# A bidirectional scan with routed experts on one core: the common mark behind the preparation is taken out, and three rows of C are read ahead of the expert rows

## The chip, the core and the metric

The kernel runs on one core of one Trainium2 chip. A core has TensorE (PE, matmuls), VectorE (DVE), ScalarE (ACT), GpSimd (POOL) and SyncE (SP), each with an instruction stream of its own, tied by semaphores. SP issues nearly all DMAs here; POOL issues the indirect ones. The metric is the device time in microseconds of one execution; the median of the runs is compared.

## The reference

The input x is 8 sequences of 512 tokens with 128 features, in float32. It is normalized per token (xn), and two branches are added to x:

```python
xn = layernorm(x)
# branch 1: two state-space scans, one forwards, one on the reversed sequence
xz = einsum('ed,bld->bel', in_proj_w, xn)           # x, z: 256 channels each
u = silu(causal_conv(x, 4 taps) + bias)             # per direction
delta = softplus(dt_proj(x_proj(u)[:8]) + dt_bias); B, C = x_proj(u)[8:24], [24:40]
h[l] = exp(delta * A) * h[l-1] + delta * B * u      # 16 states per channel
y = sum_n(h * C) + D * u;  out = y * silu(z)        # both directions added
branch1 = out_proj(out_f + out_b)
# branch 2: 16 experts, the best 4 of each token
logits = -|xn - keys|^2 + xn @ rw + rb;  top 4, softmax weights
branch2 = sum_k w_k * (w2_e @ gelu(w1_e @ xn + b1_e) + b2_e)
return x + branch1 + branch2
```

## The kernel before, in words

There is a preparation of all 8 batches, and then 8 batches of scans, each of 32 steps (`PAIRS`, q = 0 to 31).

**The preparation.** `prepare(b)` exists on ACT, PE and DVE. It makes, per batch, delta (`pos_part`, two halves), du = delta * u (`du_p`), the gate, the skip term, and the rows of B (parts) and C. These are stored to memory arrays delta_d, du_d, gate_d, skip_d, parts_d and c_d by SP (`store_prepared`, L614 and L622), and each store counts up a semaphore: delta_out, du_out, gate_out, skip_out, parts_out, c_out. Meanwhile POOL scatters the token rows to slots sorted by expert (L817).

**The arena.** Most working arrays of both phases are carved out of one array `arena`, so that the second phase writes where the first one had its arrays. `decay` (a ring of 8 steps) lies over constants, the transposed xn and weights. `c_rows` (a ring of 4) lies over weights, `mag` and, with the fourth slot and a little of the third, `pos_part` and its neighbour. The states lie over u, the rows of B and C and `fit`. The du of the second batch parity is `du_p`'s memory in part.

**The border.** At the end of `prepare(BATCH - 1)` DVE writes eight memsets into `decay` (the column where a scan starts, L1527) and marks them with decay_free, for which ACT waits ahead of its first decay. Then DVE waits for the last stores of gate, C, parts and delta, for skip_sb and du_ready, and sets one semaphore, `prepared`. It goes straight on with batch 0. SP waits for `prepared` between `read_first` and its first reads of C; POOL waits for it ahead of its batches; ACT waits for it in step 3 of batch 0 (`EMPTY_LAG - 1`). PE has waits of its own: skip_sb, parts_ready, then delta_ready and `turned` ahead of batch 0.

**SP at the border.** Behind the last stores it calls `read_first()`: it waits for POOL's scatters and reads, for two tiles of expert rows, the rows (L561, 130 KB) and their tags (L562, 2 KB). Then come `prepared`, the reads of four rows of C (`read_c`, L667; 4 KB of memory copied to all 128 partitions, 512 KB), and `batch(0)` to `batch(7)`, which begins with the read of parts for batch 1 (L539). All of these go through SP's one DMA queue.

**A batch.** For each step q:

- ACT computes two decays, exp(delta * A) (L1081), into the ring, scales the transposed du for some of the pairs (L999, `scale`), and empties PE's banks for the expert work (`empty`). The first T bank of batch 0 is emptied in step 3 (L1014).
- PE first makes the fills for DVE: L1318 for pairs that ACT has scaled, L1321 (a row of B brought to all partitions) for the others, at every second step for both j. Then come the expert events of that step (`besides`): T is the transposition of a tile's rows (L1271) and waits for `rows_in`, U0 and U1 are the up-projection (L1278), D the down-projection. Then `sum_states` transposes and sums products of step q - 4 (L1257).
- DVE multiplies a fill with du (`dbx`, L1569) and scans (L1581). Its order per four steps is fixed in `batch`: product, scan, scan, product, scan, scan, a pair of products, and so on. The third time in batch 0 it needs the two fills of step 2.
- POOL multiplies the states of a step with the row of C (L851), waiting for the scans and for `c_in`, and sends expert results by indirect DMA.

The table `FIRST_T` says that batch 0 has its T events at steps 1, 4, 7 and so on:

```python
FIRST_T = [1, 4, 7, 10, 13] + T_STEP[GROUP:]
```

PE runs in program order: fill of step 1, T of step 1, fills of step 2.

Of the kernel before, what the change touches and what calls it, by code (L numbers as in the profile page):

```python
# [15 lines left out]
BATCH, L = 8, 512  # L16
# [4 lines left out]
NH = DIN // P  # L21
ND = 2
DH = ND * NH
# [27 lines left out]
DA_RING = 8  # L51
H_RING = 8
B_RING = 4
C_RING = 4
# [239 lines left out]
def build_kernel(nc, x_in, consts_in, chan_in, inw_in, xproj_in, dtw_in, outw_in,  # L294
                 route_in, b2_in, w1_in, w2_in, out):
    with ExitStack() as ctx:
# [64 lines left out]
        def carve(n):  # L361
# [5 lines left out]
        decay = carve(DA_RING * 2 * L).rearrange("p (r j l) -> p r j l", r=DA_RING, j=2)  # L367
# [99 lines left out]
            xpad_ready z_ps z_sb v_ready u_ready xd_ps xd_sb part1_ready  # L467
            rest_ps part2_ready parts_ps parts_ready dt_ps mag_ready small_ready square_ready exp_ready
            ln_ready sum_ready fit_ready delta_ready du_ready skip_ps skip_sb gate_out c_out
            parts_out skip_out delta_out du_out decay_free prepared early_in0 early_in1 late_in0  # L470
            late_in1 skip_in0 skip_in1 decay_ready b_ready dbx_done scan_done prod_done v_prod_done summed y_free m0_ready m0_free m1_ready m1_free gelu_done
            b2_in b2_split b2_out turn_ps turned scaled
            mixed_out mixed_in sp_step pool_step acc_ready acc_last out_done"""
        s = {n: sem(n) for n in names.split()}
# [27 lines left out]
        def _(sp):  # L502
# [100 lines left out]
            def read_first():  # L603

                for g in range(TQ):
                    sp.wait_ge(scattered[g], 16 * (NT // TQ) * TOPK)
                    sp.sem_inc(s["sp_step"], 1)
                for j in range(W_RING):
                    read_rows(j, j, j)
# [48 lines left out]
                    read_down_weights()  # L658
            read_up_weights()
            store_prepared(BATCH - 1)  # L660
            read_first()
            sp.wait_ge(s["prepared"], 1)

            def read_c(b, r):
                g, d = r // ND, r % ND
# [64 lines left out]
                        n = q - MIXED_FROM  # L730
                        sp.dma_start(scanned[2 * n // BATCH][:, n % (BATCH // 2), :], mixed_d[n]).then_inc(s["mixed_in"], 16)

            for r in range(C_RING):
                read_c(0, r)

            sp.wait_ge(s["du_out"], 16 * BATCH)
            sp.wait_ge(s["skip_out"], 16 * BATCH)
# [33 lines left out]
        def _(pool):  # L771
# [47 lines left out]
                if n > 0 and n - 1 + TQ < TOPK * TQ:  # L819
                    tag(n - 1 + TQ)  # L820
            pool.wait_ge(s["acc_filled"], 16 * ACC_DMAS)
            pool.wait_ge(s["prepared"], 1)

            def sums_landed(b, before, j):

# [42 lines left out]
        def _(act):  # L868
# [204 lines left out]
            def batch(b, par, i):  # L1073
                act.wait_ge(s[f"early_in{par}"], 48 * i + 48)
                for q in range(PAIRS):
                    g, dh = q // DH, q % DH

                    wait(act, s["scan_done"], DECAYS * b + 2 * (q - DA_RING) + 2)
                    lo = 1 if dh < NH else 0
                    for j in range(2):  # L1080
                        nc.scalar.activation(decay[:, q % DA_RING, j, lo:lo + L - 1], delta[:, par, dh, lo:lo + L - 1], ACT.Exp,  # L1081
                                             scale=a_neg[:, dh, 2 * g + j:2 * g + j + 1]).then_inc(s["decay_ready"], 1)
                    if isinstance(b, int) and b == 0 and q == EMPTY_LAG - 1:
                        act.wait_ge(s["prepared"], 1)
                    if (q + PROD_AHEAD) % DH < 2:
                        g, half = (q + PROD_AHEAD) // DH, (q + PROD_AHEAD) % DH
                        if g < PAIRS // DH:
                            scale(b, g, 1, par, half)
                        elif not (isinstance(b, int) and b == BATCH - 1):
                            bank_emptied(act, s, b, "Y", 0, 1)  # L1090
                            scale(b + 1, 0, 1, 1 - par, half)
                    elif (q + PROD_AHEAD) // DH in BOTH:
                        scale(b, (q + PROD_AHEAD) // DH, 0, par, (q + PROD_AHEAD) % DH - 2)
                    besides(b, q, par)
# [17 lines left out]
        def _(pe):  # L1112
# [124 lines left out]
            for h in range(NH):  # L1237
                turn_du(ps[:, h, :], 0, h).then_inc(s["turn_ps"], 1)
            turn_b(ps[:, 2, :], 0).then_inc(s["turn_ps"], 1)
            pe.wait_ge(s["delta_ready"], ND * BATCH)  # L1240
            pe.wait_ge(s["turned"], 3)

            def sum_states(b, q, par, i):
# [61 lines left out]
            def batch(b, par, i):  # L1305
                first = isinstance(b, int) and b == 0
                pe.wait_ge(s[f"early_in{par}"], 48 * i + 48)
                for q in range(PAIRS):
                    g, d, h = q // DH, q // NH % ND, q % NH
                    for j in (1, 0):  # L1310
                        if (q, j) in FILLS:

                            wait(pe, s["scan_done"], DECAYS * b + scans_to(q - 2, j))
                            if scaled(q, j):
                                pe.wait_ge(s["scaled"], 2 * (len(SCALED) * b + SCALED.index((g, j)) + 1))
                                bank = b_ps[:, ROW[q, j], j, :]
                                for t in range(TPB):
                                    last = nc.tensor.transpose(bank[:, t * P:(t + 1) * P],  # L1318
                                                               scaled_du[scaled_slot(g, j)][:, t, h * P:(h + 1) * P], ident[:, :])
                            else:  # L1320
                                last = nc.tensor.matmul(b_ps[:, ROW[q + 1, j], j, :], sel[:, 2 * g + j, :], parts[:, par, d, :],  # L1321
                                                        start=True, stop=True)
                            last.then_inc(s["b_ready"], 1)
                    besides(b, q, par, i)
                    if not first:
                        for k in SUMS_AFTER[q]:
                            sum_states(b - 1, k, 1 - par, i if par else i - 1)
                    for k in SUMS[q]:
                        sum_states(b, k, par, i)
# [15 lines left out]
        def _(dve):  # L1345
# [138 lines left out]
            def prepare(b):  # L1484
                if b + 2 < BATCH:
                    convolve(b + 2, range(KC - 1))
                if b == 0:
                    experts_of_tiles()
                if b == 0:
                    dve.wait_ge(s["slots_zeroed"], 16 * ZERO_DMAS)  # L1490
                for d in range(ND):
                    way, n = slice(d * NH, (d + 1) * NH), ND * b + d + 1
                    dve.wait_ge(s["exp_ready"], n)
                    nc.vector.tensor_scalar(small[:, way], mag[:, way], SMALL, None, ALU.min).then_inc(s["small_ready"], 1)
                if b + 2 < BATCH:
                    convolve(b + 2, range(KC - 1, KC))
                wait(dve, s["delta_out"], 16 * b)
                for d in range(ND):
                    way, n = slice(d * NH, (d + 1) * NH), ND * b + d + 1
                    dve.wait_ge(s["square_ready"], n)  # L1500
                    dve.wait_ge(s["small_ready"], n)
                    nc.vector.scalar_tensor_tensor(fit[:, way], fit[:, way], SQ_REST, small[:, way], ALU.add, ALU.mult)\
                        .then_inc(s["fit_ready"], 1)
                    dve.wait_ge(s["ln_ready"], n)
                    dve.wait_ge(s["fit_ready"], n)
                    nc.vector.scalar_tensor_tensor(fit[:, way], ln1p[:, way], 0.0, fit[:, way], ALU.max, ALU.add)\
                        .then_inc(s["sum_ready"], 1)
                    dve.wait_ge(s["dt_ps"], n)
                    dve.wait_ge(s["sum_ready"], n)
                    nc.vector.scalar_tensor_tensor(pos_part[:, way], ps[:, DT_BANK + d * NH:DT_BANK + (d + 1) * NH, :], 0.0,  # L1510
                                                   fit[:, way], ALU.max, ALU.add).then_inc(s["delta_ready"], 1)
                for d in range(ND):
                    way, n = slice(d * NH, (d + 1) * NH), ND * b + d + 1
                    dve.wait_ge(s["delta_ready"], n)
                    dve.wait_ge(s["u_ready"], n)
                    if d == 0:
                        wait(dve, s["du_out"], 16 * b)
                    nc.vector.tensor_tensor(du_p[:, way], pos_part[:, way], u[b % U_RING][:, way], ALU.mult).then_inc(s["du_ready"], 1)
                if b == BATCH - 1:


                    dve.wait_ge(s["parts_ready"], BATCH)
                    dve.wait_ge(s["fit_ready"], ND * BATCH)
                    dve.wait_ge(s["sum_ready"], ND * BATCH)
                    for r in range(DA_RING):
                        at = 0 if r % DH < NH else L - 1
                        last = nc.vector.memset(decay[:, r, :, at:at + 1], 0.0)  # L1527
                    last.then_inc(s["decay_free"], 1)


            start = done[0]
# [9 lines left out]
                prepare(b)  # L1541


            for n in ("gate_out", "c_out", "parts_out", "delta_out"):
                dve.wait_ge(s[n], 16 * BATCH)
            dve.wait_ge(s["skip_sb"], BATCH)
            dve.wait_ge(s["du_ready"], ND * BATCH)
            dve.sem_inc(s["prepared"], 1)

            def gate_batch(b, par, i):  # L1550

# [150 lines left out]
```

## Time and profile before

| | us |
|---|---|
| median of 3 runs | 1089.65 (1088.19 to 1090.78) |
| the profiled execution | 1092.9 |
| its span, first to last instruction | 1091.1 |
| mean granted clock of TensorE | 0.947 |
| DVE busy | 1029.2 (94%) |
| ACT busy | 940.0 (86%) |
| PE busy | 932.0 (85%) |
| POOL busy | 907.3 (83%) |

Busy times are those of one profiled execution. Shares are averages over the preparation (up to about 241 us), the eight batches, and the end, in which the accumulated expert sums are added and written. DVE's largest group is the scan, L1581, 598.2 us in 512 instructions. The rows further down are from the border between preparation and batch 0, around 240 us, and from the batches behind it. Times in a timeline are microseconds from the start of the span; what stands in brackets is the idle time of the engine ahead of the line, and what ended it.

### The profile page before, as it was taken

The page shows a single profiled execution, that of the slowest core. Times are in us where ns is not written, and L with a number is a line of the kernel's source. Part 1 is how long each engine was busy: PE and PEld are TensorE (multiplying, and loading weights), DVE is VectorE, ACT ScalarE, POOL GpSimd, SP SyncE. Part 2 cuts the span into 40 slices and gives each one's busy share as a digit, 9 for nine tenths or more (in the row PEclk, how much of TensorE's full clock was granted, in tenths as well). Part 3 has the DMA queues.
Part 4 walks back from the last instruction along what each step waited for, and adds up shares of the span by engine and source line. Part 5 has one row for each costly group of instructions (what it writes and reads, how often), then busy time and mean ns, then how long its engine had stood idle before and what let it go on. Part 6 is the DMA issues. An engine that isn't in the chain of part 4 may idle for free. (4 is left out here: it accounts for less than half of the span.)

```text
span 1091.1 us, 21878 instructions
## 1 busy us (share of the span) xinstructions
PE 932.0 (85%) x5866; PEld 732.8 (67%) x5866; DVE 1029.2 (94%) x1361; ACT 940.0 (86%) x1755; POOL 907.3 (83%) x567
## 2 busy tenths in 40 slices
PE   5478888857789999989999889899999999988894
PEld 2233333326678788878878777788788878877783
DVE  7889999779999999999999989999999999988896
ACT  4258989979899999989999989899899989988950
POOL 4278888766689999999999998989999999988862
PEclk9678989778999999999999999999999999999996
DMA  9956676677566877787687767776877777666658
GB/s 305 377 191 242 241 280 226 225 267 233 177 176 181 233 197 187 205 218 196 165 225 196 201 171 219 205 192 180 238 191 185 211 210 201 164 167 170 188 114 243
DMA packets 153107, 228.87 MB, mean 210 GB/s; under 512 B 36300, under 2 KB 98028, under 8 KB 147700
## 3 DMA queue, kind: packets, MB, share of 16 engines
q1 hardware_dynamic: 125844, 208.39, 60.0%
q0 software_dynamic: 27136, 19.02, 12.3%
q8 instruction: 51, 0.84, 0.3%
q14 instruction: 76, 0.62, 0.2%
HBM read 161.84 MB, written 69.64 MB: 212 GB/s over the span
## 5 line engine op out<-in xcount | busy, mean ns | idle before, releaser
L1581 DVE TENSOR_TENSOR_SCAN arena<-arena,ps 128x512 f32<-128x512 f32 x512 | 598.2, 1202 | 2.8 <-issue 1.4
L851 POOL TENSOR_TENSOR arena<-arena 128x1024 f32<-128x1024 f32 x246 | 527.0, 2472 | 44.5 <-DVE arena L1581 44.4
L1081 ACT ACTIVATE arena<-delta,a_neg 128x511 f32<-128x511 f32 x512 | 341.3, 728 | 6.3 <-DVE arena L1581 3.2
L836 POOL DMA_INDIRECT acc_d<-yrows,tags x160 | 253.1, 1582 | 46.5 <-issue 36.8
L1257 PE MATMUL ps<-ident,arena 128*128 128x128 f32 x2048 | 270.6, 276 | 3.5 <-DVE arena L1589 3.5
L1569 DVE TENSOR_TENSOR ps<-du,ps 128x512 f32<-128x512 f32 x352 | 232.8, 677 | 18.0 <-PE ps L1321 15.9
L1257 PEld LDWEIGHTS ps<-ident,arena 128*128 128x128 f32 x2048 | 233.0, 142 | 15.6 <-DVE arena L1589 4.0
L817 POOL DMA_INDIRECT slots_d<-arena,pos x128 | 148.4, 1159 | 37.1 <-issue 35.1
L1286 PE MATMUL ps<-w,arena 128*128 128x128 f32 x1248 | 174.6, 283 | 3.0 <-ACT arena L1049 3.0
L1286 PEld LDWEIGHTS ps<-w,arena 128*128 128x128 f32 x1248 | 154.4, 192 | 12.8 <-issue 3.8
L1278 PE MATMUL ps<-rowsT,w 128*128 128x256 f32 x640 | 155.8, 387 | 8.3 <-ACT arena L1031 7.6
L999 ACT ACTIVATE arena<-arena 128x256 f32<-128x256 f32 x320 | 145.4, 510 | 0.0
L1278 PEld LDWEIGHTS ps<-rowsT,w 128*128 128x128 f32 x640 | 119.2, 193 | 28.7 <-ACT arena L1031 9.2
L1020 ACT ACTIVATE arena<-ps,w 128x256 f32<-128x256 f32 x312 | 123.4, 477 | 5.4 <-PE ps L1278 5.1
L1318 PE MATMUL ps<-ident,arena 128*128 128x128 f32 x640 | 94.5, 278 | 16.5 <-DVE arena L1581 12.5
L1026 ACT ACTIVATE yrows<-ps,tags 128x128 f32<-128x128 f32 x160 | 49.9, 365 | 49.2 <-PE ps L1288 34.4
L1318 PEld LDWEIGHTS ps<-ident,arena 128*128 128x128 f32 x640 | 74.0, 143 | 21.2 <-DVE arena L1581 13.7
L1049 ACT ACTIVATE arena<-arena 128x1024 f32<-128x1024 f32 x78 | 79.1, 1054 | 0.2
L1321 PE MATMUL ps<-parts,sel 128*128 128x512 bf16 x176 | 59.3, 390 | 12.9 <-DVE arena L1581 12.9
L1271 PE MATMUL ps<-ident,rows 128*128 128x128 f32 x160 | 33.3, 290 | 37.1 <-ACT arena L1020 22.5
L1477 DVE SCALAR_TENSOR_TENSOR arena<-arena,chan 128x512 f32<-128x512 f32 x96 | 64.7, 740 | 0.0
L1271 PEld LDWEIGHTS ps<-ident,rows 128*128 128x128 f32 x160 | 18.3, 141 | 52.8 <-ACT arena L1020 23.6
(154 smaller groups left out, 911.6 us busy)
## 6 DMA issues: line engine op xcount, KB each, us to landing
arena<-c_d SPq DMA_DIRECT2D x128, 512.0 KB, 4.2
w<-w_dram SPq DMA_DIRECT2D x80, 258.0 KB, 3.1
w<-w_dram SPq DMA_DIRECT2D x80, 256.0 KB
rows<-slots_d SPq DMA_DIRECT2D x80, 130.0 KB
slots_d<-delta SPq DMA_DIRECT2D x5, 2015.0 KB, 18.9
delta_d<-arena SPq DMA_DIRECT2D x8, 1024.0 KB, 4.9
du_d<-delta SPq DMA_DIRECT2D x8, 1024.0 KB, 7.9
delta<-delta_d SPq DMA_DIRECT2D x8, 1024.0 KB, 7.0
```

Source lines behind the costliest of these rows:

```text
L817: pool.indirect_dma_start(slots_d, bass.IndirectOffsetOnAxis(ap=pos[:, t * TOPK + k:t * TOPK + k + 1], axis=0), xn[:, t, :], None).then_in ...
L836: pool.indirect_dma_start(acc_d[j % W_RING], bass.IndirectOffsetOnAxis(ap=tags[:, j, a, 0:1].bitcast(I32), axis=0), yrows[:, j % W_RING, a ...
L851: nc.gpsimd.tensor_tensor(state[:, q % H_RING], state[:, q % H_RING], c_rows[:, r % C_RING], ALU.mult).then_inc(s["prod_done"], 1)
L999: last = nc.scalar.activation(scaled_du[scaled_slot(g, j)][:, t, :], duT[:, par, t, :], ACT.Identity, scale=bT[:, par, t, n:n + 1])
L1020: last = nc.scalar.activation(hidden[hidden_slot(b, j)][:, c, :], bank[:, f * S:(f + 1) * S], ACT.Identity, bias=w1[:, j % W_RING, FF + c: ...
L1081: nc.scalar.activation(decay[:, q % DA_RING, j, lo:lo + L - 1], delta[:, par, dh, lo:lo + L - 1], ACT.Exp, scale=a_neg[:, dh, 2 * g + j:2 ...
L1257: last = nc.tensor.matmul(y_ps[:, h, t * P:(t + 1) * P], state[:, q % H_RING, j, t * P:(t + 1) * P], ident[:, :], is_transpose=True, start ...
L1278: last = nc.tensor.matmul(bank[:, f * S:(f + 1) * S], w1[:, slot, c * P:(c + 1) * P], rowsT[:, :], start=True, stop=True)
L1286: nc.tensor.matmul(bank[:, a * P:(a + 1) * P], kept[:, c, a * P:(a + 1) * P], w2[:, slot, c, :], start=c == 0, stop=False)
L1318: last = nc.tensor.transpose(bank[:, t * P:(t + 1) * P], scaled_du[scaled_slot(g, j)][:, t, h * P:(h + 1) * P], ident[:, :])
L1569: nc.vector.tensor_tensor(b_ps[:, ROW[q, j], j, :], du[:, par, q % DH, :], b_row, ALU.mult)\
L1581: nc.vector.tensor_tensor_scan(state[:, q % H_RING, j, way], decay[:, q % DA_RING, j, way], b_ps[:, ROW[q, j], j, way], 0.0, ALU.mult, ALU ...
```

## The change

The semaphore `prepared` goes. Each engine waits for the semaphores of those arrays whose memory it writes next:

- DVE does its memsets ahead of the two du products of the last batch, behind skip_sb and parts_ready, and waits for c_out, parts_out and du_ready before batch 0. It no longer waits for gate_out and delta_out.
- ACT waits for gate_out, c_out, parts_out, delta_out and du_ready in step 3 of batch 0.
- PE waits for delta_ready behind the fills of step 0 instead of ahead of them.
- POOL has no wait there.
- SP waits for c_out, decay_free and du_ready, reads three rows of C, then calls `read_first` (scatters, rows and tags of two tiles), waits for delta_out and reads the fourth row of C.

```diff
@@ SP
             store_prepared(BATCH - 1)
-            read_first()
-            sp.wait_ge(s["prepared"], 1)
...
-            for r in range(C_RING):
+            sp.wait_ge(s["c_out"], 16 * BATCH)
+            sp.wait_ge(s["decay_free"], 1)
+            sp.wait_ge(s["du_ready"], ND * BATCH)
+            for r in range(C_RING - 1):
                 read_c(0, r)
+            read_first()
+            sp.wait_ge(s["delta_out"], 16 * BATCH)
+            read_c(0, C_RING - 1)
@@ POOL
             pool.wait_ge(s["acc_filled"], 16 * ACC_DMAS)
-            pool.wait_ge(s["prepared"], 1)
@@ ACT, batch
                     if isinstance(b, int) and b == 0 and q == EMPTY_LAG - 1:
-                        act.wait_ge(s["prepared"], 1)
+                        for n in ("gate_out", "c_out", "parts_out", "delta_out"):
+                            act.wait_ge(s[n], 16 * BATCH)
+                        act.wait_ge(s["du_ready"], ND * BATCH)
@@ PE
-            pe.wait_ge(s["delta_ready"], ND * BATCH)
             pe.wait_ge(s["turned"], 3)
...
+                    if first and q == 0:
+                        pe.wait_ge(s["delta_ready"], ND * BATCH)
                     besides(b, q, par, i)
@@ DVE, prepare
+                if b == BATCH - 1:
+                    dve.wait_ge(s["skip_sb"], BATCH)
+                    dve.wait_ge(s["parts_ready"], BATCH)
+                    for r in range(DA_RING):
+                        at = 0 if r % DH < NH else L - 1
+                        last = nc.vector.memset(decay[:, r, :, at:at + 1], 0.0)
+                    last.then_inc(s["decay_free"], 1)
                 for d in range(ND):
...
                     nc.vector.tensor_tensor(du_p[:, way], ...).then_inc(s["du_ready"], 1)
-                if b == BATCH - 1:
-                    dve.wait_ge(s["parts_ready"], BATCH)
-                    dve.wait_ge(s["fit_ready"], ND * BATCH)
-                    dve.wait_ge(s["sum_ready"], ND * BATCH)
-                    (the same memsets)
@@ DVE, ahead of the batches
-            for n in ("gate_out", "c_out", "parts_out", "delta_out"):
+            for n in ("c_out", "parts_out"):
                 dve.wait_ge(s[n], 16 * BATCH)
-            dve.wait_ge(s["skip_sb"], BATCH)
             dve.wait_ge(s["du_ready"], ND * BATCH)
-            dve.sem_inc(s["prepared"], 1)
```

## Rows read from the trace of the kernel before

**Rows 1.** Stretches: busy of PE, PEld, DVE, ACT, POOL; PE clock, DMA share, GB/s.
```profile
243.10:248.80 5.70, 2.29 (x6) 1.24 (x7) 5.67 (x7) 5.70 (x12) 0.00 (x0) 0.50 0.94 257
248.80:343.00 94.20, 79.09 (x539) 68.06 (x537) 93.72 (x106) 85.81 (x175) 73.88 (x40) 0.95 0.65 189
343.00:443.00 100.00, 92.65 (x681) 81.36 (x682) 98.59 (x110) 94.92 (x194) 94.27 (x53) 1.00 0.75 200
```
**Rows 2.** Timeline of DVE at the border: start us, us, line, operation, count.
```profile
238.63 2.35 DVE L1518 TENSOR_TENSOR delta<-arena 128x1024 f32<-128x1024 f32 x2
240.93 0.17 DVE L1527 MEMSET arena<- 128x2 f32 x8
243.13 0.70 DVE L1569 TENSOR_TENSOR ps<-du,ps 128x512 f32<-128x512 f32 x1 [2.02 <-issue]
...
248.80 1.27 DVE L1569 TENSOR_TENSOR ps<-du,ps 128x512 f32<-128x512 f32 x2
```
**Rows 3.** Timeline of SP's DMA issues at the border.
```profile
238.81 0.35 SPq L614 DMA_DIRECT2D delta_d<-arena  x1
241.07 0.33 SPq L614 DMA_DIRECT2D du_d<-delta  x1
243.26 0.41 SPq L561 DMA_DIRECT2D rows<-slots_d  x1
...
245.57 1.89 SPq L667 DMA_DIRECT2D arena<-c_d  x4
```
**Rows 4.** Timeline of PE at the border.
```profile
239.68 0.63 PE L1321 MATMUL ps<-parts,sel 128*128 128x512 bf16 x1
...
246.41 0.69 PE L1271 MATMUL ps<-ident,rows 128*128 128x128 f32 x2 [5.25 <-DMA tags<-slots_d]
246.89 1.06 PE L1321 MATMUL ps<-parts,sel 128*128 128x512 bf16 x2
```
**Rows 5.** Timeline of ACT at the border.
```profile
232.93 0.99 ACT L956 COPY gatedT<-ps 128x1024 f32<-128x1024 f32 x1
...
241.14 3.78 ACT L1081 ACTIVATE arena<-delta,a_neg 128x511 f32<-128x511 f32 x6 [2.94 <-DVE arena L1527]
...
246.84 0.90 ACT L999 ACTIVATE arena<-arena 128x256 f32<-128x256 f32 x2
247.64 0.35 ACT L1014 COPY rowsT<-ps 128x256 f32<-128x256 f32 x1
```
**Rows 6.** Timeline of POOL: its first products with C.
```profile
251.36 9.84 POOL L851 TENSOR_TENSOR arena<-arena 128x1024 f32<-128x1024 f32 x5 [11.88 <-DVE arena L1581]
```
**Rows 7.** DMA packets moved in 241:245, 244:245, 245:247, 247:248 and 247:256.4.
```profile
DMA packets 233, 1.58 MB, mean 396 GB/s; under 512 B 32, under 2 KB 32, under 8 KB 48
...
DMA packets 48, 0.39 MB, mean 393 GB/s; under 512 B 0, under 2 KB 0, under 8 KB 0
...
DMA packets 1113, 0.31 MB, mean 154 GB/s; under 512 B 592, under 2 KB 1104, under 8 KB 1113
...
DMA packets 56, 0.23 MB, mean 229 GB/s; under 512 B 0, under 2 KB 0, under 8 KB 56
...
DMA packets 715, 2.36 MB, mean 251 GB/s; under 512 B 80, under 2 KB 80, under 8 KB 713
```
**Rows 8.** Issue to landing (last column, us): du's store, C's first read, C's third.
```profile
du_d<-delta SPq DMA_DIRECT2D x1, 1024.0 KB, 4.7
...
arena<-c_d SPq DMA_DIRECT2D x1, 512.0 KB, 5.6
...
arena<-c_d SPq DMA_DIRECT2D x1, 512.0 KB, 8.0
```
**Rows 9.** DVE's waits, 243 to the end: total us, times, longest us.
```profile
DVE ps L1569 <- PE ps L1321: 15.9, 25, 1.7
DVE gated L1555 <- PE ps L1257: 6.2, 8, 2.6
...
DVE arena L1581 <- ACT arena L1081: 1.0, 2, 0.5
```

More of the change, by code:

```diff
@@ L469, in build_kernel @@
             ln_ready sum_ready fit_ready delta_ready du_ready skip_ps skip_sb gate_out c_out
-            parts_out skip_out delta_out du_out decay_free prepared early_in0 early_in1 late_in0
+            parts_out skip_out delta_out du_out decay_free early_in0 early_in1 late_in0
             late_in1 skip_in0 skip_in1 decay_ready b_ready dbx_done scan_done prod_done v_prod_done summed y_free m0_ready m0_free m1_ready m1_free gelu_done
@@ L1518, in prepare @@
                     nc.vector.tensor_tensor(du_p[:, way], pos_part[:, way], u[b % U_RING][:, way], ALU.mult).then_inc(s["du_ready"], 1)
-                if b == BATCH - 1:
-                    dve.wait_ge(s["parts_ready"], BATCH)
-                    dve.wait_ge(s["fit_ready"], ND * BATCH)
-                    dve.wait_ge(s["sum_ready"], ND * BATCH)
[L1525 to L1528, printed above, removed]
             start = done[0]
```

## The prediction

> **What bounds the kernel now.** I read the table by stretches first [rows 1]. In the hundred microseconds from 343 on DVE is busy for 98.6, in the 94.2 us behind 248.8 for 93.7. DVE is the engine that sets the pace of the eight batches, and it has next to no idle time in the first one. So what counts for the end is the time at which DVE gets going with batch 0; a microsecond lost or won there is carried through. Two idle pieces lie at this border. The first is DVE's own: its last work of the preparation ends at 241.10, its first product of batch 0 starts at 243.13, 2.02 us later, with no releaser shown [rows 2]. That is the wait for the store of delta, issued at 238.81 [rows 3], the last of the arrays in DVE's list ahead of `prepared`. The second is PE's: it waits 5.25 us, until 246.41, for the first expert rows, since its first T event stands in step 1, in program order ahead of the two fills of step 2 [rows 4] (the profile puts the wait down to the tags, read with the rows). DVE doesn't feel it: the fills (L1321, two in 1.06 us from 246.89) are done by 247.95, the first by some 247.5, and DVE's third product (L1569, a pair) takes it at 248.80 [rows 2, 4]. So the slack of PE's row wait against DVE is 1.3 us, and anything that moves the rows' landing by more than that moves DVE.
>
> **The start of DVE, ACT and PE.** The eight memsets (0.17 us in all, 60 ns each) go ahead of the two du products: these end at 240.98 + 0.17 = 241.15 instead of 240.98, and ACT, which waits for the memsets, can start its decays at 238.63 + 0.17 + 0.05 = 238.85 instead of 241.14 [rows 2, 5]. The added wait for skip_sb costs nothing: that copy ended at 233.92 [rows 5]. DVE's waits for gate_out and delta_out go; the stores of c_out and parts_out stand in SP's order ahead of that of delta, and are older. Its first product can start at 241.15 + 0.1 = 241.25: fill (0, 0) was done at 240.31, the first decays would be at 238.85 + 1.3 = 240.15 [rows 4, 5]. That is 1.88 us earlier. ACT's five waits before its step 3 work have behind them the empty of T and all decays from step 4; ACT gets there 5.7 us after its start (from 241.14 to the scaling at 246.84 [rows 5]), now at 244.55, when delta's store (3.9 us to landing from 238.81) has landed at 242.7. So nothing. PE's wait for delta_ready moves behind the fills of step 0; what they win is hidden by DVE, which needs the last of them at 241.25, and behind the wait stand only step 1's fill and the T that waits for its rows far longer. If the story ended here, DVE would reach its third product at 248.80 - 1.88 = 246.92, and then wait for the fill.
>
> **The order on SP's queue.** Before, SP issues behind du's store (241.07): rows, tags, rows, tags (from 243.26), then four reads of C from 245.57 (1.89 us for the four), then parts [rows 3]. After, du_ready comes 0.17 later, du's store goes at 241.24, and three reads of C are issued at once, 0.47 us each, by 243.0. Ahead of these three stand waits for c_out, decay_free (238.85) and du_ready (which du's store has waited for), all past. Ahead of the rows stands only the wait for POOL's scatters, in both kernels, so their issue time stays near 243.3. Behind the rows the wait for delta_out (242.7) is past when the fourth C comes, at 245.6; what stands behind it, the read of parts for batch 1, is issued no later than before. But the rows are now queued behind three times 512 KB of C, 1.57 MB. What does that do? The packets tell [rows 7]. From 244 to 245 all 48 packets are 8 KB or more: the rest of du's store. From 245 to 247 there are 1113 packets, 1104 of them under 2 KB: the two tiles' rows and tags. From 247 to 248 all 56 are under 8 KB and none under 2 KB: C. Du's store still had bytes when the rows had been issued for 1.7 us, and C none before 247 though issued from 245.57 [rows 3]. The queue serves in the order of issue, with hardly an overlap.
>
> How long three reads of C hold the queue: their packets began at 247.0, the third (issued 245.57 + 2 x 0.47 = 246.5, 8.0 us to landing) landed at 254.5 [rows 3, 8]. Du's store landed 0.7 to 0.8 us behind its last packet (241.07 + 4.7 = 245.8 against 245.0), so the stream of three took 254.5 - 0.75 - 247.0 = 6.8 us. After: du's packets end at 245.0 + 0.17 = 245.2, C takes until 252.0, and the first tile's rows and tags need, as before, 246.41 - 245.0 = 1.4 us until PE starts on them. PE's T starts at 253.4, not 246.41. The first fill is ready 1.1 us later (247.5 - 246.41), so DVE's third product starts at 253.4 + 1.1 = 254.5 in place of 248.80.
>
> **Sum:** + 5.7 us. The 1.88 us at the start are inside it; they become idle time at the third product, which would be 254.5 - 246.9 = 7.6 us. POOL's earlier C (its first product started at 251.36, when C landed, long after the first scans [rows 6]) buys nothing, because DVE was not waiting for POOL in this stretch (its longest idle pieces of the batches are for fills and for the gate [rows 9]). ACT can't run ahead either: the copy of the transposed rows (247.64 [rows 5]) stands in its step 3 behind PE's T. The granted clock of TensorE is at the lower of its two levels, 0.50, from 243.1 to 248.8 already, after PE's idle time from 241.2 on [rows 1, 4]; a longer idle time finds it there too, so I add nothing.
>
> **Bounds.** The queue's time is the open term. Below: C at the pace of the stores from 241 to 245, 396 GB/s [rows 7]: 1.57 / 0.396 = 4.0 us, T at 250.6, sum + 2.9. Above: three times C's first read (251.2 - 0.75 - 247.0 = 3.4 us each, 10.3): T at 256.9, sum + 9.2. I take 6.8, the burst of the same reads, issued alike, in the same place. Neither end reaches below nothing; for that the order of the queue itself has to be wrong (rival A).
>
> The Trainium skill, "DMA: Bandwidth & Descriptors", section "Bandwidth", gives 341 GB/s for a 1 MB transfer. By an estimate from this page three reads of C would take 4.6 us and the sum would be + 3.5. This case's row shows 251 GB/s over the burst [rows 7], and the measurement decides.
>
> **Rivals.** (A) *The rows aren't held up, faster.* If the rows' packets pass beside C's, PE's T stays at 246.41, the first fill at 247.5, and DVE starts it there: 248.80 - 247.5 = 1.3 us saved, 1088.4. The wait that ends last would be PE's on rows_in either way. The mechanism has a turning point: DVE's change is T + 1.1 - 248.8, so T later than 247.7 makes the kernel slower. For it: C and rows have different destinations, and only the record of one burst speaks for the order. Against: the clean borders between packet sizes.
> The same page, section "Queues, rings and completion order", says that an engine takes the descriptors of one ring in order, but that completion is not in order of issue for an issuing engine; the second half would be this rival, and the packets of this trace show the first.
> (B) *The lag of PE and ACT joins in.* T and all behind it move by 7.0 us, DVE by only 5.7; the 1.3 us of slack that PE and ACT had over DVE are used up. If a later fill or decay of batch 0 had less slack (DVE waits 0.5 us at most for decays, 1.7 for fills [rows 9]), the sum is 7.0, 1096.7. Against: decays run steps ahead of the scans.
> (C) *The loss is made good later.* DVE idles in the steady part: 15.9 us in 25 waits for fills, 6.2 us in 8 for the sums [rows 9]. If these were slack in the pipeline that a late start uses up, the end would not move: 1089.7. Against: all engines start late together, and these waits come back once per batch, made by the order within it.
>
> **Numbers.** The profiled execution of before took 1092.9 us around its span of 1091.1; the runs have a median of 1089.65, 3.25 below. A shift of the start is the same in both: a profiled span of about 1096.8 and a median of 1089.65 + 5.7 = 1095.4. Main forecast 0.70 (1092.5 to 1098.9 by the bounds), B 0.10, A 0.12, C 0.08. No change means within 0.2%, 2.2 us, about what a measurement of this kernel can tell. Slower 0.80, same 0.08, faster 0.12. The range is 1090.5 to 1098.7: it leaves out A, most of C and the uppermost end.
>
> **What would show it.** After: DVE's first product near 241.3, ACT's first decay near 238.9, three C issues from 241.6, rows still from 243.3. Then small packets only from about 252, PE's first transpose of rows (L1271) at 253.4, waiting some 12 us for tags, and DVE idle for some 7.6 us in front of its third product, put down to PE's fill. POOL's first product near 249.4 (C 4.2 us behind its first packet). From there to the end each stretch as before, shifted. It is wrong if rows land before 247.7, if DVE's stall is there but batch 1 starts no later than before, or if the small packets come among C's.

## The result: 0.38% slower

The changed kernel takes 1095.8 us (median of 8 runs, 1092.58 to 1098.57), the kernel before 1090.22 (8 runs, 1088.19 to 1093.54). The ratio is 1.0038 with a 95% interval of 1.0021 to 1.0056; from 1090.22 that is + 4.1 us, from + 2.3 to + 6.1. The two medians differ by 5.6 us, which lies inside the interval. A second set, with 12 and 35 runs, gave 1.0030 (1.0007 to 1.0053).

One thing has to be known for reading profiles of this kernel. The preparation takes a different time in each execution: over 14 profiles of this kernel and its variants the last du product of DVE ended between 240.4 and 245.7 us. The end varies as well. So I take times of the border from that point, "behind du". Three kernels were profiled twice: the two profiles agree within 0.4 us at DVE's third product, and at the gate of batch 0 within 0.1 us for two of them and 1.1 us for the third. In the kernel before it is 240.98, in the changed one 241.31.

The timeline of DVE in the changed kernel answers to [rows 2]:

```profile
238.86 0.12 DVE L1523 MEMSET arena<- 128x2 f32 x7
238.95 1.22 DVE L1531 TENSOR_TENSOR delta<-arena 128x1024 f32<-128x1024 f32 x1
...
240.09 1.22 DVE L1531 TENSOR_TENSOR delta<-arena 128x1024 f32<-128x1024 f32 x1
241.50 0.69 DVE L1570 TENSOR_TENSOR ps<-du,ps 128x512 f32<-128x512 f32 x1 [0.19 <-issue]
...
244.93 2.32 DVE L1582 TENSOR_TENSOR_SCAN arena<-arena,ps 128x512 f32<-128x512 f32 x2
254.12 1.29 DVE L1570 TENSOR_TENSOR ps<-du,ps 128x512 f32<-128x512 f32 x2 [6.87 <-PE ps L1325]
```

The 2.02 us of idle time ahead of the first product have shrunk to 0.19. Two products and two pairs of scans later DVE stands still for 6.87 us, and what ends it is PE's fill. The third product is 12.81 behind du; before, it was 7.82.

SP's issues, which answer to [rows 3]:

```profile
241.40 0.33 SPq L614 DMA_DIRECT2D du_d<-delta  x1
241.84 2.78 SPq L665 DMA_DIRECT2D arena<-c_d  x3
244.98 0.60 SPq L561 DMA_DIRECT2D rows<-slots_d  x1
245.63 0.74 SPq L562 DMA_DIRECT2D tags<-slots_d  x1
```

PE, ACT and POOL, which answer to [rows 4 to 6]:

```profile
252.97 0.69 PE L1275 MATMUL ps<-ident,rows 128*128 128x128 f32 x2 [12.07 <-DMA tags<-slots_d]
253.44 1.06 PE L1325 MATMUL ps<-parts,sel 128*128 128x512 bf16 x2
```
```profile
239.07 3.78 ACT L1084 ACTIVATE arena<-delta,a_neg 128x511 f32<-128x511 f32 x6 [0.68 <-DVE arena L1523]
...
253.69 0.37 ACT L1017 COPY rowsT<-ps 128x256 f32<-128x256 f32 x1 [8.02 <-PE ps L1275]
```
```profile
248.63 3.95 POOL L854 TENSOR_TENSOR arena<-arena 128x1024 f32<-128x1024 f32 x2 [8.96 <-DMA arena<-c_d]
```

PE waits 12.07 us for the tags where it waited 5.25. ACT did start earlier, and then stood 8.02 us behind PE's transposition. POOL had C 2.7 us earlier and nothing came of it.

The packets of the changed kernel in the stretches 244 to 245, 246 to 250, 250 to 252 and 252 to 253, which answer to [rows 7]:

```profile
DMA packets 32, 0.26 MB, mean 262 GB/s; under 512 B 0, under 2 KB 0, under 8 KB 0
...
DMA packets 311, 1.16 MB, mean 289 GB/s; under 512 B 29, under 2 KB 29, under 8 KB 311
...
DMA packets 865, 0.68 MB, mean 340 GB/s; under 512 B 374, under 2 KB 747, under 8 KB 865
...
DMA packets 459, 0.36 MB, mean 365 GB/s; under 512 B 234, under 2 KB 373, under 8 KB 459
```

The small packets of rows and tags, which ran from 245 to 247 before, are now seen from 250 to 253, behind those of C. A tile's 130 KB of rows come in 256 packets of some 520 B, so between 512 B and 2 KB: of these the stretch 246 to 250 has none (29 and 29), and 250 to 253 has all 512 of the two tiles (373 and 139). The stretches, which answer to [rows 1], in the same columns:

```profile
243.10:254.50 11.40, 1.53 (x5) 0.96 (x6) 4.53 (x6) 3.38 (x8) 3.95 (x2) 0.50 0.99 309
254.50:343.00 88.50, 72.17 (x499) 62.86 (x505) 88.50 (x99) 81.98 (x168) 65.25 (x35) 0.97 0.60 176
343.00:443.00 100.00, 91.57 (x672) 81.10 (x680) 98.59 (x111) 95.23 (x194) 94.34 (x52) 1.00 0.74 200
```

Behind 254.5 DVE has no idle time at all in batch 0 (88.50 of 88.50), so nothing can be caught up there. The first half of batch 0's gate (it stands in DVE's order early in batch 1) comes at 351.27 before and 356.04 after:

```profile
351.27 0.67 DVE L1555 TENSOR_TENSOR gated<-ps,gate 128x512 f32<-128x512 f32 x1
...
356.04 0.67 DVE L1556 TENSOR_TENSOR gated<-ps,gate 128x512 f32<-128x512 f32 x1
```

### The profile page after: what moved, and what is told of

Same layout as the page of the kernel before. It is cut to its first block and busy times, and to the rows that moved or that the text cites. A ratio compares the mean times of both kernels' runs of the same rounds, so it can differ in the third digit from the quotient of the medians.

```text
span 1092.2 us, 21806 instructions
## 1 busy us (share of the span) xinstructions
PE 924.1 (85%) x5794; PEld 730.2 (67%) x5866; DVE 1029.2 (94%) x1361; ACT 940.8 (86%) x1755; POOL 905.8 (83%) x567
## 5 line engine op out<-in xcount | busy, mean ns | idle before, releaser
L1570 DVE TENSOR_TENSOR ps<-du,ps 128x512 f32<-128x512 f32 x352 | 233.1, 678 | 22.2 <-PE ps L1325 10.3
L1325 PE MATMUL ps<-parts,sel 128*128 128x512 bf16 x104 | 38.6, 386 | 14.3 <-DVE arena L1582 11.8
```

Of the source, the lines that this page charges most:

```text
L1570: nc.vector.tensor_tensor(b_ps[:, ROW[q, j], j, :], du[:, par, q % DH, :], b_row, ALU.mult)\
```

## The experiments

My theory: the loss is made of two links, the rows' packets behind those of C, and PE's first T, ahead of the fills of step 2 in program order. Rivals: the separate waits or the moved memsets; the late issue; any read of C ahead costs the whole wait; a loss that the end takes back.

### Do the parts add up?

Three kernels: the changed one again, the changed one with only SP's order taken back, and the kernel before with only SP's order changed.

```diff
# c0_rows_first, from the changed kernel
-            for r in range(C_RING - 1):
-                read_c(0, r)
             read_first()
+            for r in range(0, C_RING - 1):
+                read_c(0, r)
             sp.wait_ge(s["delta_out"], 16 * BATCH)
# order_only, from the kernel before: SP has the changed kernel's lines, all else as before
-            read_first()
-            sp.wait_ge(s["prepared"], 1)
```

Expected of the repeat:

> The changed kernel itself, once more, so that its end can be compared with that of the kernel before in a second pair of profiles. In the first pair the third product pair of DVE came 5.3 us later, batch 1's gate 4.8 us, the last batch's gate 2.9 us and the end only 1.1 us later. Theory (the shift is carried to the end, the tail scatters from execution to execution): the median is 4.5 to 5.5 us above that of before, 1094.7 to 1095.7, and in this profile the shift at the end is again another number than 1.1. Rival (the last batch has slack that takes back most of a late start): the median is 1 to 2 us above before, 1091.2 to 1092.2, and the shift shrinks again in the last batch by 3 to 4 us.

Measured: 1095.43, ratio 1.0030. From du, the third product came at 12.65 and batch 0's gate at 114.64 (12.81 and 114.73 in the first profile), and this span was 1097.2, not 1092.2: the small difference of the first pair of spans was chance. The theory's numbers hold; the interval is too wide to exclude that a microsecond or two are taken back in the last batch.

> The changed kernel with only SP's order taken back: the expert rows and tags are read ahead of all four rows of C; all waits are those of the changed kernel. Theory (the three reads of C ahead of the rows are the loss): PE's first transposition of rows some 5.5 us behind the issue of du's store, as before; DVE's third product pair 1.1 us behind it, about 1.2 us earlier than in the kernel before; median 1089.0, 6 us below the changed kernel. Rival (the separate waits or the memsets moved ahead of du cost the time): the time stays near 1095, and DVE idles by more than 4 us elsewhere in batch 0. Rival (the reads of C slow whatever comes, in either order): third product late by 2 us or more.

Measured: 1089.36 against 1091.97, ratio 0.9977 (0.9958 to 0.9996), and 6.1 us below the 1095.43 of the changed kernel in the same set.

```profile
241.73 0.70 DVE L1570 TENSOR_TENSOR ps<-du,ps 128x512 f32<-128x512 f32 x1 [0.19 <-issue]
248.00 1.29 DVE L1570 TENSOR_TENSOR ps<-du,ps 128x512 f32<-128x512 f32 x2 [0.52 <-PE ps L1325]
```

The early start is there, du having ended at 241.54, and the third product is 6.46 behind du, 1.36 earlier than in the kernel before. That is the slack of 1.3 that the rows of before gave. The separate waits cost nothing and win 1.4 us at this point (1.0 in a second profile of this kernel, in which SP waited longer for POOL's last scatter and issued the rows 2.88 behind du instead of 2.02).

> The kernel before, with SP's order alone changed: three reads of C ahead of the expert rows (SP waits for c_out, decay_free and du_ready in place of the common mark); DVE, ACT, PE and POOL as before, the common mark included. Theory: DVE starts at its old time, 2 us idle behind the preparation, and then idles some 5 us ahead of its third product pair, which starts at the same time as in the changed kernel (about 12.7 us behind the issue of du's store); median 1095.3, like the changed kernel. Rival (early start and early reads collide, so that the loss needs both): 1091 to 1092.

Measured: 1095.66, ratio 1.0030 (1.0009 to 1.0051).

```profile
243.36 0.70 DVE L1573 TENSOR_TENSOR ps<-du,ps 128x512 f32<-128x512 f32 x1 [2.03 <-issue]
254.07 1.29 DVE L1573 TENSOR_TENSOR ps<-du,ps 128x512 f32<-128x512 f32 x2 [4.96 <-PE ps L1325]
```

With the common mark kept, the third product comes 12.87 behind du, as in the changed kernel. The idle time is only divided otherwise, 2.03 + 4.96 in place of 0.19 + 6.87. So the order alone is the loss, and the waits' gain is swallowed by it.

### How much per row of C?

One, two and four rows of C ahead of the expert rows (`for r in range(1)` and so on ahead of `read_first()`, the rest behind it; four need delta_out first).

> The changed kernel with one row of C ahead of the expert rows instead of three (a dose between none and three). Measured from the end of the du products, DVE's third product pair came at 6.5 us with none ahead and at 12.7 to 12.8 with three. Theory (the rows' packets stand behind those of C in one queue, so each read of C adds its own streaming time): C's first read alone streams in some 3.4 us, so the third pair comes at about 9.5 to 10 us. Rival (any read of C ahead of the rows costs the whole wait, for instance because its completion is awaited): 12.7 us. Rival (the late issue of the rows is the cause, not the queue: in the changed kernel SP issued them 1.7 us later than forecast): about 7 us.

> The same with two rows of C ahead. Theory (queue order, each read adds what it streams): the third pair at about 11 to 11.5 us behind the end of the du products, between the one for one row and the 12.7 for three. Rival (all or nothing): 12.7. Rival (issue time): about 7.5.

> The changed kernel with all four rows of C ahead of the expert rows (SP waits for delta_out first). With none, one, two and three ahead, DVE's third pair came at 6.5, 8.5, 10.8 and 12.7 us behind the end of the du products. Theory (each read of 512 KB takes its time ahead of the rows, 2.1 us): 14.8 us. Rival (later reads go faster, as the fourth did in the burst of the kernel before, some 1.3 us apart): 14.0 us.

DVE's third product in these three kernels, du having ended at 244.48, 244.38 and 245.73:

```profile
253.01 1.29 DVE L1572 TENSOR_TENSOR ps<-du,ps 128x512 f32<-128x512 f32 x2 [2.60 <-PE ps L1327]
```
```profile
255.18 1.29 DVE L1572 TENSOR_TENSOR ps<-du,ps 128x512 f32<-128x512 f32 x2 [4.87 <-PE ps L1327]
```
```profile
259.92 1.29 DVE L1569 TENSOR_TENSOR ps<-du,ps 128x512 f32<-128x512 f32 x2 [8.25 <-PE ps L1324]
```

| rows of C ahead | third product behind du | gate of batch 0 behind du |
|---|---|---|
| 0 | 6.46 (again: 6.86) | 108.39 (109.52) |
| 1 | 8.53 | 111.03 |
| 2 | 10.80 | 112.82 |
| 3 | 12.81 (12.65) | 114.73 (114.64) |
| 4 | 14.19 | 116.53 |

A dose and its response: 2.07, 2.27, 2.01 and 1.38 us, each known to some 0.4. That refutes "all or nothing". It refutes "issue time" too: with one row ahead SP issued the first expert rows 1.26 behind du, earlier than with none (2.02), and the third product still came 2.07 later. My number for one row (9.5 to 10) was too high: the 3.4 us from C's first read in the kernel before isn't what one read adds. For four rows the rival was nearer (14.0; I had 14.8), the last read adds less. That step is not a clean dose: with the wait for delta_out ahead of them, SP issued the reads of C from 1.74 behind du instead of 0.53. The single times of these, 1092.3, 1099.1 and 1099.88, have no interval and say little beside a spread of several microseconds.

### Is it the queue or the engines behind it?

```diff
# c3_act_queue, ACT in step 1 of batch 0; SP's queue keeps rows, tags and the fourth C
+                    if isinstance(b, int) and b == 0 and q == 1:
+                        act.wait_ge(s["c_out"], 16 * BATCH)
+                        act.wait_ge(s["du_ready"], ND * BATCH)
+                        for r in range(C_RING - 1):
...
+                            nc.scalar.dma_start(c_rows[:, r].rearrange("p j l -> p (j l)"),
+                                                src.to_broadcast([P, 2 * L])).then_inc(c_in[r], 16)
```

> The changed kernel, but the three early reads of C are issued by ACT in its step 1 of batch 0 and so stand in ACT's own DMA queue; SP's queue holds du's store, rows and tags, and the fourth read of C. Same transfers, nearly the same time of issue, same 16 DMA engines. Theory (the order within one queue holds the rows back): the rows pass part of C, PE's first transposition comes 2 to 4 us earlier than in the changed kernel (about 8 to 9.5 us behind the end of the du products instead of 11.6), the third pair at 9 to 10.5 us, and the median lies 1.5 to 3.5 us below the changed kernel. Rival (the engines' capacity alone decides, whichever queue): the third pair stays at 12.7 us and the median at 1095. ACT loses about 1.5 us for three issues, which its lead over DVE covers.

Measured: 1095.8 against 1089.32, ratio 1.0058 (1.0038 to 1.0077). PE's T came 11.70 behind du (11.66 in the changed kernel), the third product at 12.85. Here the rival was right. ACT had issued its three reads of C at 240.81, with du's store (240.82) and 3.3 us ahead of the rows. The queues in the stretches 247 to 249, 249 to 250 and 250 to 251 (q10 is ACT's, with C; q1 is SP's; packets, MB, share of 16 engines):

```profile
DMA packets 179, 0.57 MB, mean 285 GB/s; under 512 B 40, under 2 KB 40, under 8 KB 179
q10 hardware_dynamic: 163, 0.57, 94.5%
q1 hardware_dynamic: 16, 0.00, 0.5%
...
q10 hardware_dynamic: 96, 0.36, 90.2%
q1 hardware_dynamic: 57, 0.03, 10.0%
...
q1 hardware_dynamic: 582, 0.17, 71.2%
q10 hardware_dynamic: 52, 0.15, 37.8%
```

SP issued the first rows at 244.14, and du's store was through by 247, yet for more than two microseconds nearly nothing of q1 moved while C had the engines for 94.5%. So a queue of their own for the reads of C doesn't let the rows pass. "The queue serves in the order of issue" was a good description of one queue, and too narrow as a cause. What fits all of these runs is that the bytes issued ahead went first, whichever of the two queues held them (one profile of this kernel). Of the 40 small packets from 247 to 249 none has the size of a row. Why the rows didn't share the engines with C, as du's store did, stays open.

### Cutting the other link

PE's first T behind the fills of step 2: `FIRST_T` with 2 in place of 1 (T stands behind the fills of its step), then all four first T a step later, with the rows first and with C first.

```diff
-FIRST_T = [1, 4, 7, 10, 13] + T_STEP[GROUP:]
+FIRST_T = [2, 4, 7, 10, 13] + T_STEP[GROUP:]     # t_step2_rows_first
+FIRST_T = [2, 5, 8, 11, 13] + T_STEP[GROUP:]     # t_2_5_8_rows_first and _again; c3_t_2_5_8 with C ahead
```

> The changed kernel with rows ahead of C as in the kernel before, and PE's first T event in step 2 of batch 0 instead of step 1, which is behind the fills that DVE's third product pair needs. Theory (PE's program order is the link between the rows' landing and DVE): no idle time ahead of the third pair; DVE keeps all of its earlier start, 1.6 to 1.9 us; median 1088.5, below both kernels. Rival (something else holds the third pair, such as a clock that is low or the bank still in use): the third pair stays where it is with T in step 1, and the time is that of the kernel with rows ahead of C, 1089.0 or more.

Measured: 1091.31, ratio 0.9997 (0.9974 to 1.0019): a miss for the total, not for the place. The third pair had no wait, 5.86 behind du; but a new one stood at step 8:

```profile
270.20 0.70 DVE L1570 TENSOR_TENSOR ps<-du,ps 128x512 f32<-128x512 f32 x1 [1.70 <-PE ps L1322]
```
```profile
267.18 0.41 PE L1275 MATMUL ps<-ident,rows 128*128 128x128 f32 x2 [4.22 <-DMA tags<-slots_d]
```

The first is DVE, the second PE. U0 and U1 had moved by a step too, with them the reload of the third tile's rows, while its T had stayed in step 7. The stall had moved on by two tiles, and the gate came at 109.56 behind du, 1.2 later than with T in step 1.

> Rows ahead of C and the separate waits, as in the best kernel so far, with PE's T events of batch 0 in steps 2, 5, 8, 11, 13 instead of 1, 4, 7, 10, 13. With only the first T moved to step 2, DVE's third pair started without a wait (5.9 us behind the end of the du products), but DVE idled 1.70 us at step 8, where PE stood in front of the third tile's rows for 4.2 us. Theory (each T has to stand behind the fills that DVE takes next): with all four moved by a step, both pieces of idle time are gone, the gate of batch 0 comes 107.8 to 108.0 us behind the end of the du products (110.3 in the kernel before, 108.4 with rows first alone), and the median is 1088.7. Rival (the expert rows are late by more than a step, so that the wait moves to step 10): DVE idles over 1 us there and the gate comes at 109 us or later.

Measured: 1088.95 against 1089.32, ratio 0.9995 (0.9976 to 1.0015). Both idle pieces are gone, the gate comes 108.12 behind du, 2.2 us ahead of the kernel before. The times alone don't show it.

> The changed kernel, three rows of C still ahead of the expert rows, but PE's T events of batch 0 in steps 2, 5, 8, 11, 13. The rows land as late as in the changed kernel (PE's first transposition about 11.6 us behind the end of the du products). Theory (the loss is the product of the late rows and PE's program order, and either one alone costs little): DVE's third pair starts at 5.9 us without a wait; PE stands in front of the rows behind the fills of step 2, and DVE, which needs the fills of step 4 some 6.8 us after the third pair (12.7 us), gets them at about 14 and waits 1 to 1.5 us; the gate of batch 0 comes at 109.3 us instead of 114.7; median 4 us or more below the changed kernel, 1090 to 1091. Rival (the late rows cost the same wherever T stands, since all expert work of batch 0 shifts and meets DVE's fills later): the gate at 112 us or later, the median at 1093 to 1095.

Measured: 1091.47, as before (ratio 0.9998, 0.9979 to 1.0017), with C still ahead of the rows. DVE and then PE:

```profile
257.65 0.69 DVE L1570 TENSOR_TENSOR ps<-du,ps 128x512 f32<-128x512 f32 x1 [0.63 <-PE ps L1325]
262.24 2.33 DVE L1582 TENSOR_TENSOR_SCAN arena<-arena,ps 128x512 f32<-128x512 f32 x2 [1.07 <-PE ps L1322]
```
```profile
255.65 0.69 PE L1275 MATMUL ps<-ident,rows 128*128 128x128 f32 x2 [7.62 <-DMA tags<-slots_d]
```

The rows are as late as ever, T 11.40 behind du. DVE loses 0.63 + 1.07 = 1.70 us to them instead of 6.87, and the gate is at 110.04 behind du (109.3 expected) against 114.73. So both links are needed for most of the loss. The late rows are not free even then: with the same T events and the rows first the gate is at 108.12, 1.9 us earlier.

### The two best, side by side

> The kernel with rows ahead of C and the separate waits, once more, side by side with the one whose T events are moved. In its first runs it was 0.23% faster than before (interval 0.04 to 0.42%). Theory (its batch 0 is 1.9 us shorter from the end of the du products to the gate, 108.4 against 110.3, and that is carried to the end): the median is 1.5 to 2.5 us below that of before. Rival (the first comparison was luck of the preparation and of the end, which vary by some 3 us each between executions): no difference.

> Rows ahead of C, separate waits, T events in steps 2, 5, 8, 11, 13, once more. Its gate of batch 0 came 108.1 us behind the end of the du products, 0.3 us ahead of the kernel with T in step 1. Theory: the median lies 0.3 us below that one, which is less than the runs can tell, and 1.5 to 2.5 us below before. Rival (moved expert work costs more in the end than the 0.3 us): 1 us or more above the kernel with T in step 1.

Measured against 1091.59 for the kernel before: rows first 1090.19, ratio 0.9983 (0.9967 to 0.9999); rows first with T in 2, 5, 8, 11, 13 1088.41, ratio 0.9974 (0.9958 to 0.9989). Two sets of runs of the first lie below 1 with their intervals. Of the second, one does and one (0.9995) doesn't; its gate was 108.12 and 108.13 behind du, the first one's 108.39 and 109.52. Both are at or below the kernel before and clearly below the changed one; the second kernel is the better by its profiles (no idle time of DVE ahead of the third product, against 0.52 and 0.93), by times it can't be told from the first.

## Why the prediction was right

- *What sets the pace.* Right. DVE has 88.50 of 88.50 us in batch 0 behind the stall, and the gate of batch 0 carries the shift: + 4.4 us behind du, from a third product that is 5.0 later.
- *The start.* Right. The first product starts 0.19 behind du instead of 2.15; the forecast was 241.25 with du ending at 241.15, so 0.10 behind. ACT's first decay came at 239.07, forecast 238.85, and no wait that was added is seen.
- *The place of the new wait.* Right: the third product, put down to PE's fill, with PE's T in front of the tags behind it. 6.87 us against 7.6 forecast.
- *The issue times.* Wrong, without effect. The rows were issued at 244.98, not 243.3, because three issues of C took 2.78 us instead of 1.4. The 1.6 us that SP waited for POOL's scatter ahead of the rows in the kernel before are gone in their place. At 244.98 nearly all of C was still ahead: from 244 to 245 all 32 packets were of 8 KB or more, du's store.
- *The size.* The mis-sized term is the stream of three reads of C, 6.8 us. T came 11.66 behind du with three rows ahead and 5.31 with none: 6.35, that is 2.1 for each 512 KB (5.79 and 1.9 by the second profiles of both). I had taken the time in which the third of four reads landed, in which what stood behind it had a share: from 247.0 to 253.75 the queue moved 1.94 MB in the kernel before, three reads are 1.57 (the fourth and the read of parts stood behind them). The bounds 4.0 and 10.3 held it. So 5.5 behind du by forecast became 5.0 at the third product. To the gate it became 4.4: the kernel before has 0.48 us of DVE idle time at 283.36, the profiles of the changed one have none there, some of the other kernels do (0.31 to 0.49), and what decides it is open. Forecast + 5.7 us (0.52%), measured 0.38% (0.21 to 0.56%). That the two medians differ by 5.6 us, next to the forecast, is in part luck: batch 0 was shifted by 4.4, and the medians of the second set differ by 3.5.
- *The clock.* Right: put at nothing. TensorE was granted 0.50 over the stall and 0.97 behind it (0.95 before), and from the third product to the gate it took 101.92 us against 102.47.
- *Rivals.* A (the rows pass beside C) is refuted, even for two queues. B (the lag joins in) is refuted by batch 0 without idle time. C (made good later) is not seen up to batch 2: its gate is 4.4 us later behind du as well (552.89 and 557.65). In the last batches the two profiles of the changed kernel stray more than the question is worth, the last gate 832.4 and 834.4 behind du against 829.8, and the end of the span 850.9 and 853.2 against 850.1, a shift of 0.8 or of 3.1. Two other kernels with a third product as late, `order_only` and `c3_act_queue`, had their last gate 831.1 and 833.9 behind du and their end at 850.1 and 854.4, so the end strays by 4 us for one and the same start. Whether a microsecond or two are given back there is open; the medians, 5.6 and 3.5 apart, don't decide it.

## What to carry to other kernels

When reads are put ahead of others on a busy set of DMA engines, list what waits for the ones that now come later, and in whose program order they stand: PE's wait of 5.25 us was free, and would have been until it grew by more than the 1.3 us that its next output had to spare. Count the bytes issued ahead of a transfer; a second queue didn't help here. And before a stall is cut off at its head, look at which wait is next: moving one T moved the stall to the third tile, moving all of them removed it.

## What the hardware showed unexpectedly

- Reads of C that stood in ACT's queue held back reads of rows in SP's queue: 16 packets of q1 in two microseconds, with q10 at 94.5%, though the rows had been issued by SP 3 us before. Du's store, in the same queue as the rows, had shared the engines with C until 247 (landing 7.1 us behind its issue, 5.4 in the changed kernel).
- A read of 512 KB, 4 KB copied to 128 partitions, added 2.0 to 2.3 us to what stood behind it, 230 to 260 GB/s, for the first three reads, and 1.4 for a fourth. By my estimate from issue and landing the first read of the burst in the kernel before took 3.4.
- Three DMA issues of SP took 2.78 us in the changed kernel (1.89 for four before), with du's store just issued ahead of them.
- The preparation ended within 240.4 to 245.7 us over the 14 profiles, and at 240.37 and 244.10 in two of one and the same program, which is nearly as much as the effect under study. Times behind a mark near the change repeated within 0.4 us at the third product, and within 1.1 at the gate.
